# Second-choice sends one group behind the first ones, and blocks closed without GpSimd's DRAIN, in a two-FFN mixture-of-experts layer on one core

## The chip, the cores and the metric

The program runs on one core of one Trainium2 chip. The time is the device time of one execution in microseconds (us); of several executions the median counts. Lower is better.

## The reference

The input is x, 8 x 1024 tokens of 128 features. Three residual steps follow one another, and the first and the last are the same FFN with the same weights:

```python
x = x + 0.5 * ffn(layernorm(x))
x = x + attn(layernorm(x))
x = x + 0.5 * ffn(layernorm(x))

def ffn(x):                                   # x: 8192 x 128, 16 experts, top 2
    scores = softmax(x @ gate_w + gate_b)
    top_vals, top_idx = top_k(scores, 2)
    cw = (one_hot(top_idx, 16) * top_vals[..., None]).sum(axis=1)
    a = silu(x @ w1[e] + b1[e]) * (x @ w3[e] + b3[e])         # 176 wide, for each e
    y = einsum('teh,ehd,te->td', a, w2, cw) + cw @ b2
    z = silu(x @ sw1 + sb1) * (x @ sw3 + sb3) @ sw2 + sb2     # shared expert, 352 wide
    return y + z
```

The attention is linear: q and k go through elu + 1, kv = sum over the tokens of k v for each of 16 heads of 8, out = q kv, and a projection.

## The kernel before, in words

The 8192 tokens are 64 tiles of 128 tokens, in 8 groups of 8 tiles. They stay in SBUF (`xa`) from beginning to end. The program has six stages, each in a `phase`: front 0, experts 0, attention, front 1, experts 1, combine. Each stage is one `nc.Block()`, in which every engine has its own instruction stream and waits on semaphores by hand. At the end of a block all engines meet. Then `phase` clears the stage's semaphores (L71, `clear_and_free_semaphores`, done by GpSimd) and all engines meet again (L72, `all_engine_barrier`).

**front** (twice, n = 0 and 1) normalizes the tokens, computes the gate, finds both experts of each token, computes the shared expert on TensorE, and sends each token's row of 130 floats (128 features, a destination and a weight) to the table `xs` in HBM, once for the first choice and once for the second. There a region belongs to each expert. A send is one indirect DMA of 128 rows, issued by GpSimd (POOL) at L316; a group of one choice is eight of them. Both fronts issue 128. Both choices are sent from the same rows of SBUF, `xrow`: the first choice goes with destination `dest0` and weight 0.5/sum, and only when all eight first sends of the group have landed may VectorE (DVE) overwrite these two columns. That is `rewrite(g)` (L444 to L452): a wait on `sent0`, two small instructions (L449, L451), and the semaphore `rewrote`.

DVE, ScalarE, TensorE and POOL run on in steps s = -1 to 9. In step s they do the gate of group s and the shared expert of group s - 1, which is cut in six parts m. DVE's step (L526 to L563) reads, in this order: `shifts(s+1)` (L374, needs GpSimd's `scales`), `largest(s)`, `indices(s)`, three of six `gates` with `outs` between them, `hot(s)` (L409), `moments(s+2)`, `gates`, `sums(s)`, `variances(s+2)` (L369 is its last), `gates`, `outs`, `places(s)`, whose last instruction writes the slots of the group (L442), `gates`, `low` twice (L457), and as its last `rewrite(s-2)`.

GpSimd's stream in a front (L326 to L341): three `scales` (L323, one power of -1/2 of the variances of a group; it waits for `variances`), and then for each g the first sends of group g (wait on the slots of g), `scales(g+3)`, and the second sends of group g - 2 (wait on `rewrote`). Only after all sends have landed does it come to the end of the block. SyncE (SP) loads weights in front 0, and at the end copies 16 padding tiles in `xs` (L269).

**experts** takes 144 tiles of 128 rows in pairs: SP loads them (L860), TensorE transposes and multiplies, and GpSimd scatters each result tile to `ys` with one indirect DMA (L873). **attention** and **combine** read `ys` with DMAs of SP (L1060, L1265).

A block begins at L204 (front), L846 (experts), L1056 (attention) and L1259 (combine): what the program issues at the block's end carries these line numbers in the profile.

Of the kernel before, what the change touches and what calls it, by code (L numbers as in the profile page):

```python
# [32 lines left out]
GROUPS = 8  # L33
# [107 lines left out]
def front(nc, k, sb, ps, n, xa, xs, w=None):  # L141

    with phase(nc) as sem, ExitStack() as ctx:
# [57 lines left out]

            return slice(g * GT, (g + 1) * GT)

        with nc.Block() as block:  # L204
            @block.sync
            def _(sp):
                if n == 0:
# [64 lines left out]
            @block.gpsimd  # L272
            def _(pool):
                if n == 0:
                    pool.memset(k.ident[:], 0.0)
                    pool.memset(k.tri[:], 1.0)
                    pool.memset(k.blockdiag[:], 1.0)
                    pool.memset(k.onesb[:], 1.0)
                    pool.memset(k.nhalf[:], -0.5)
                    pool.memset(k.ones_e[:], 1.0).then_inc(tail, 1)  # L280
                    pool.wait_ge(tail, 1)
                    pool.affine_select(out=k.ident[:], in_=k.ident[:], compare_op=ALU.not_equal,
                                       fill=1.0, base=0, pattern=[[-1, P]], channel_multiplier=1
                                       ).then_inc(consts, 1)
                    pool.affine_select(out=k.tri[:], in_=k.tri[:], compare_op=ALU.is_ge, fill=0.0,
                                       base=-1, pattern=[[1, P]], channel_multiplier=-1)
                    heads = k.blockdiag[:].rearrange("p (a c) -> p a c", c=HEAD_DIM)
                    pool.affine_select(out=heads, in_=heads, compare_op=ALU.is_ge, fill=0.0,
                                       base=0, pattern=[[-HEAD_DIM, D // HEAD_DIM], [0, HEAD_DIM]],
                                       channel_multiplier=1).then_inc(consts, 1)  # L290
                    pool.wait_ge(consts, 2)
                    pool.affine_select(out=heads, in_=heads, compare_op=ALU.is_ge, fill=0.0,
                                       base=HEAD_DIM - 1,
                                       pattern=[[HEAD_DIM, D // HEAD_DIM], [0, HEAD_DIM]],
                                       channel_multiplier=-1)
                    pool.iota(k.iota_e[:], pattern=[[1, E]], base=0, channel_multiplier=0,
                              allow_small_or_imprecise_dtypes=True)
                    pool.iota(k.iota_j[:], pattern=[[P, 2]], base=0, channel_multiplier=1,
                              allow_small_or_imprecise_dtypes=True)
                    pool.iota(k.region[:], pattern=[[REGION, E]], base=0, channel_multiplier=0,  # L300
                              allow_small_or_imprecise_dtypes=True).then_inc(consts, 1)
                    pool.memset(k.zero[:], 0.0)
                    pool.memset(k.pad_tail[:], 0.0).then_inc(consts, 1)
                    pool.wait_ge(consts, 4)
                    pool.iota(k.pad_tail[:, :, 0:1].bitcast(I32).rearrange("p j a -> p (j a)"),
                              pattern=[[P, PADS]], base=TOKENS * K_TOP, channel_multiplier=1
                              ).then_inc(tail, 1)
                pattern = [[2 * GT * P, GROUPS], [2, GT]]
                pool.iota(dest0, pattern=pattern, base=0, channel_multiplier=2 * GT)
                pool.iota(dest1[:].rearrange("p (b i) -> p b i", i=GT), pattern=pattern, base=1,  # L310
                          channel_multiplier=2 * GT).then_inc(dests, 1)
                pool.wait_ge(dests, 1)

                def send(g, q, done):
                    for i in range(g * GT, (g + 1) * GT):
                        pool.indirect_dma_start(  # L316
                            xs, bass.IndirectOffsetOnAxis(slot[:, q, i:i + 1], 0), xrow[:, i, :],
                            None).then_inc(done, 16)

                def scales(g):  # L320
                    pool.wait_ge(var, g + 1)
                    wait(pool, xhr, 2 * (g - 2))
                    pool.tensor_tensor(rs[g % 3][:], ve[g % 2][:], k.nhalf[:], ALU.pow  # L323
                                       ).then_inc(rstd, 1)

                for g in range(3):  # L326
                    scales(g)
                for g in range(GROUPS + 2):
                    if g < GROUPS:
                        pool.wait_ge(slots, g + 1)  # L330
                        pool.wait_ge(weighted, g + 1)
                        pool.wait_ge(xhr, 2 * g + 2)
                        pool.sem_inc(passed, 1)
                        send(g, 0, sent0[g % 3])
                    if g + 3 < GROUPS:
                        scales(g + 3)
                    if g >= 2:
                        pool.wait_ge(rewrote, g - 1)
                        pool.sem_inc(passed, 1)
                        send(g - 2, 1, sent1)  # L340
                pool.wait_ge(sent1, 16 * TILES)  # L341

            @block.vector
            def _(dve):
# [181 lines left out]
                def step(s):  # L526
                    m, new, gating = 6 * (s - 1), s + 2 < GROUPS, 0 <= s < GROUPS
                    if 0 <= s < GROUPS - 1:
                        shifts(s + 1)
                    if gating:  # L530
                        largest(s)
                        indices(s)
                    gates(m)
                    if s == GROUPS:
                        tables()
                    gates(m + 1)
                    outs(2 * (s - 1) - 1)
                    if s == GROUPS:
                        tables_out()
                    gates(m + 2)  # L540
                    if gating:
                        hot(s)
                    if new:
                        moments(s + 2)
                    gates(m + 3)
                    if gating:
                        sums(s)
                    if new:
                        variances(s + 2)
                    gates(m + 4)  # L550
                    outs(2 * (s - 1))
                    if gating:
                        places(s)
                    gates(m + 5)
                    if gating:
                        if n == 0:
                            weight_low(2 * s)
                        low(2 * s)
                        low(2 * s + 1)
                        if n == 0:  # L560
                            weight_low(2 * s + 1)
                    if s >= 2:
                        rewrite(s - 2)  # L563

                if n == 0:
                    for r in range(4):
# [27 lines left out]
                for s in range(1, GROUPS + 2):  # L594
                    step(s)
# [215 lines left out]
def experts(nc, k, sb, ps, n, xs, ys):  # L811

    with phase(nc) as sem, ExitStack() as ctx:
# [28 lines left out]
            for j in range(TAIL, last):  # L843
                step(j, j)

        with nc.Block() as block:  # L846
            @block.sync
            def _(sp):
                def load(first, free):
# [160 lines left out]
def attention(nc, k, sb, ps, xa, ys):  # L1010
# [3 lines left out]
    with phase(nc) as sem, ExitStack() as ctx:  # L1014
# [19 lines left out]
        s = {m: sem(f"t_{m}") for m in names}  # L1034
# [18 lines left out]
        v_of = p_kv[:].rearrange("p a (t n) -> p (a t) n", n=2 * D)[:, :, D:2 * D]  # L1053
        q_of = p_q[:].rearrange("p a n -> p (a n)")

        with nc.Block() as block:  # L1056
            @block.sync
            def _(sp):
                def load(g, gv):
# [193 lines left out]
def combine(nc, sb, rs, ys, out):  # L1253

    with phase(nc) as sem, ExitStack() as ctx:
        yt = [sb(f"c_yt{r}", [P, GT, 2 * D], ctx=ctx) for r in range(4)]
        in_ready = [sem(f"c_in{r}") for r in range(GROUPS)]
        half, ysum, stored = sem("c_half"), sem("c_ysum"), sem("c_stored")
        with nc.Block() as block:  # L1259
            @block.sync  # L1260
            def _(sp):
                for g in range(GROUPS):
                    if g >= 4:
                        sp.wait_ge(ysum, g - 3)
                    sp.dma_start(yt[g % 4][:], ys[:, g]).then_inc(in_ready[g], 16)  # L1265
                sp.wait_ge(stored, 16 * GROUPS)

            @block.vector
            def _(dve):
                for g in range(GROUPS):  # L1270
                    dve.wait_ge(in_ready[g], 16)
                    dve.tensor_tensor(rs[:, g * GT:(g + 1) * GT], rs[:, g * GT:(g + 1) * GT], yt[g % 4][:, :, 0:D], ALU.add  # L1272
                                      ).then_inc(half, 1)
                    dve.wait_ge(half, g + 1)
                    dve.tensor_tensor(rs[:, g * GT:(g + 1) * GT], rs[:, g * GT:(g + 1) * GT], yt[g % 4][:, :, D:2 * D], ALU.add  # L1275
                                      ).then_inc(ysum, 1)

            @block.scalar
            def _(act):
                for g in range(GROUPS):  # L1280
                    act.wait_ge(ysum, g + 1)
                    act.dma_start(out[:, g], rs[:, g * GT:(g + 1) * GT]).then_inc(stored, 16)
# [26 lines left out]
```

## Time and profile before

| | us |
|---|---|
| median of 3 runs | 1052.64 |
| lowest, highest | 1049.37, 1054.99 |
| profiled execution, its own time | 1053.46 |
| its span, first to last instruction | 1051.7 |
| TensorE busy | 803.1 (76% of the span) |
| GpSimd busy | 590.6 (56%) |
| VectorE busy | 588.3 (56%) |
| ScalarE busy | 468.7 (45%) |

In the profile, times are from the start of the span. A line of a timeline gives the start and the duration in us, the engine, the line of the kernel, the operation and the tiles, and in brackets the idle time of the engine before it with what ended it ("issue" stands for idle time for which the profile shows no releaser).
### The profile page before, as it was taken

The numbers are of one execution on the slowest core, as the hardware profiler recorded it, in microseconds if no ns is written. First come the engines' busy times: TensorE is split into PE (matmuls) and PEld (weight loads), VectorE is DVE, ScalarE is ACT, GpSimd is POOL, SyncE is SP. The second block draws the span as 40 slices with busy tenths as digits, with TensorE's granted clock in tenths as the row PEclk, the third lists the DMA queues.
The fourth block names the chain that finished last, engine by engine and source line by source line (L and its number), as shares of the span: only waits on it lengthen the run. The fifth ranks groups of instructions, "written<-read, shape, count | busy, mean of one in ns | idle before, by whom it ended". The sixth has DMA issues, their size and how long they took to land. (4 is left out here: it accounts for less than half of the span.)

```text
span 1051.7 us, 20394 instructions
## 1 busy us (share of the span) xinstructions
PE 803.1 (76%) x5408; PEld 718.9 (68%) x5409; DVE 588.3 (56%) x1989; ACT 468.7 (45%) x926; POOL 590.6 (56%) x600
## 2 busy tenths in 40 slices
PE   2899999607999999328989489999810999999910
PEld 2677787507999999326777468877710999999910
DVE  6577766404555555256885477776600555555526
ACT  3466564104555555134664256575200555555500
POOL 2446777753777777532220146677774477776730
PEclk9999999858999999757999679998965999999965
DMA  9812221312333333232200001111231333333339
GB/s 276 118 38 60 66 63 51 95 43 77 101 103 101 103 104 96 68 133 81 80 0 1 0 22 34 40 49 49 61 88 39 89 101 101 103 101 103 94 132 374
DMA packets 82819, 90.42 MB, mean 86 GB/s; under 512 B 20414, under 2 KB 69451, under 8 KB 80715
## 3 DMA queue, kind: packets, MB, share of 16 engines
q1 hardware_dynamic: 63052, 45.42, 16.9%
q0 software_dynamic: 17408, 35.95, 10.2%
q10 hardware_dynamic: 2304, 8.39, 2.0%
q8 instruction: 26, 0.43, 0.2%
q14 instruction: 29, 0.24, 0.1%
HBM read 47.46 MB, written 44.37 MB: 87 GB/s over the span
## 5 line engine op out<-in xcount | busy, mean ns | idle before, releaser
L873 POOL DMA_INDIRECT ys<-e_y,e_x x288 | 275.8, 958 | 139.8 <-issue 87.8
L316 POOL DMA_INDIRECT xs<-f_xrow,f_slot x256 | 252.8, 987 | 87.6 <-issue 75.3
L992 PE MATMUL e_py<-w,e_at 97*128 (+1 forms) x1152 | 152.2, 274 | 0.0
L992 PEld LDWEIGHTS e_py<-w,e_at 97*128 97x128 f32 (+1 forms) x1152 | 139.9, 191 | 0.2 <-issue 0.2
L917 ACT ACTIVATE e_xth<-e_px 128x256 fp32r<-128x256 f32 x144 | 55.2, 384 | 171.4 <-PE e_px L956 171.4
L897 DVE TENSOR_TENSOR e_a<-e_pu,e_sil 128x352 f32<-128x352 f32 x144 | 75.5, 525 | 96.9 <-ACT e_sil L923 91.6
L956 PE MATMUL e_px<-ident,e_x 128*128 128x128 f32 x288 | 57.7, 282 | 90.7 <-DMA e_x<-xs 86.4
L904 DVE TENSOR_SCALAR e_y<-e_py,e_x 128x128 f32<-128x128 f32 x288 | 87.8, 346 | 58.0 <-PE e_py L992 57.9
L756 PEld LDWEIGHTS f_pz<-sw,f_gated 128*128 128x128 f32 (+1 forms) x768 | 102.6, 195 | 9.3
L649 ACT ACTIVATE f_sil<-f_phg,sb 128x512 f32<-128x512 f32 (+1 forms) x96 | 64.7, 685 | 97.9 <-PE f_phg L742 97.6
L468 DVE SCALAR_TENSOR_TENSOR f_gated<-f_phg,sb,f_sil 128x512 f32<-128x512 f32 (+1 forms) x96 | 71.7, 747 | 63.8 <-ACT f_sil L649 54.4
L923 ACT ACTIVATE e_sil<-e_pu 128x352 f32<-128x352 f32 x144 | 66.7, 463 | 89.9 <-PE e_pu L969 89.9
L967 PE MATMUL e_pu<-w13h,e_xth 128*128 x288 | 106.7, 370 | 0.0
L756 PE MATMUL f_pz<-sw,f_gated 128*128 128x128 f32 (+1 forms) x768 | 102.7, 278 | 0.0
L956 PEld LDWEIGHTS e_px<-ident,e_x 128*128 128x128 f32 x288 | 36.0, 145 | 94.9 <-DMA e_x<-xs 89.7
L742 PE MATMUL f_phg<-f_xth,sw13h 128*128 128x512 f32 (+1 forms) x192 | 89.7, 467 | 10.3 <-ACT f_sil L649 9.1
L969 PE MATMUL e_pu<-w13h,e_xtl 128*128 x288 | 93.7, 325 | 0.0
L968 PE MATMUL e_pu<-w13l,e_xth 128*128 x288 | 93.6, 325 | 0.0
L929 ACT ACTIVATE e_at<-e_pa 96x512 f32<-96x512 f32 x144 | 85.5, 594 | 1.6 <-PE e_pa L979 1.6
L979 PE MATMUL e_pa<-ident,e_a 128*96 128x128 f32 x576 | 86.2, 272 | 0.0
L742 PE MATMUL f_phg<-f_xtl,sw13h 128*128 128x512 f32 (+1 forms) x192 | 79.3, 413 | 0.0
L742 PE MATMUL f_phg<-f_xth,sw13l 128*128 128x512 f32 (+1 forms) x192 | 78.8, 410 | 0.0
(160 smaller groups left out, 1431.7 us busy)
## 6 DMA issues: line engine op xcount, KB each, us to landing
e_x<-xs SPq DMA_DIRECT2D x288, 65.0 KB
t_yt<-ys SPq DMA_DIRECT2D x8, 1024.0 KB, 4.9
c_yt<-ys SPq DMA_DIRECT2D x8, 1024.0 KB, 10.4
ys<-e_y,e_x POOLq DMA_INDIRECT x288
xa<-in_attn_x ACTq DMA_DIRECT2D x8, 512.0 KB, 10.3
xs<-f_xrow,f_slot POOLq DMA_INDIRECT x256, 2.4
out<-xa ACTq DMA_DIRECT2D x8, 512.0 KB
f_raw<-in_ffn_w SPq DMA_DIRECT2D x32, 88.0 KB
```

Source lines behind the costliest of these rows:

```text
L316: pool.indirect_dma_start(xs, bass.IndirectOffsetOnAxis(slot[:, q, i:i + 1], 0), xrow[:, i, :], None).then_inc(done, 16)
L742: last = pe.matmul(p_hg[(2 * m + g) % 3][0:wd], w_[:, cols], x_[c % 3][:], start=q == 0, stop=q == 2)
L756: last = pe.matmul(p_z[c % 2][:, tok], gated[c % 2][0:wd, f, tok], k.sw2[0:wd, f], start=f == 0 and q == 0, stop=f == 2, skip_group_check= ...
L873: pool.indirect_dma_start(ys, bass.IndirectOffsetOnAxis(xin[r][:, t, D:D + 1].bitcast(I32), 0), y[r][:, t, :], None).then_inc(sent[r], 16)
L904: last = dve.tensor_scalar(y[s][:, t], p_y[j % 2][:, t * D:(t + 1) * D], xin[s][:, t, D + 1:D + 2], None, ALU.mult)
L929: act.activation(at[r][0:A0], p_a[0:A0], ACT.Copy).then_inc(turned, 1)
L956: last = pe.transpose(p_x[:, t * P:(t + 1) * P], xin[s][:, t, 0:D], k.ident[:])
L967: pe.matmul(o, xth[r][:, tok], k.w13h[:, cols], start=True, stop=False)
L968: pe.matmul(o, xth[r][:, tok], k.w13l[:, cols], start=False, stop=False)
L969: last = pe.matmul(o, xtl[r][:, tok], k.w13h[:, cols], start=False, stop=True)
L979: last = pe.transpose(p_a[0:A0, q * P:(q + 1) * P], a[r][:, t, o:o + A0], k.ident[:])
L992: last = pe.matmul(p_y[r][:, t * D:(t + 1) * D], at[r][0:rows_, q], w2, start=c == 0, stop=c == 1, skip_group_check=True)
```

## The change

In GpSimd's stream the second sends of group g - 1, in place of g - 2, follow the first sends of group g. The loop is one turn shorter. In DVE's step `rewrite(s-2)` stands ahead of `hot(s)` and no longer at the end. All four `nc.Block()` get `no_gpsimd_drain=True`: at the block's end GpSimd issues no DRAIN, and the engines meet by semaphores alone. `phase`, with its clearing of semaphores and the barrier behind it, is as before.

```diff
-        with nc.Block() as block:
+        with nc.Block(no_gpsimd_drain=True) as block:
...
                 for g in range(3):
                     scales(g)
-                for g in range(GROUPS + 2):
+                for g in range(GROUPS + 1):
                     if g < GROUPS:
                         pool.wait_ge(slots, g + 1)
                         pool.wait_ge(weighted, g + 1)
...
                         send(g, 0, sent0[g % 3])
                     if g + 3 < GROUPS:
                         scales(g + 3)
-                    if g >= 2:
-                        pool.wait_ge(rewrote, g - 1)
+                    if g >= 1:
+                        pool.wait_ge(rewrote, g)
                         pool.sem_inc(passed, 1)
-                        send(g - 2, 1, sent1)
+                        send(g - 1, 1, sent1)
                 pool.wait_ge(sent1, 16 * TILES)
...
                     gates(m + 2)
+                    if s >= 2:
+                        rewrite(s - 2)
                     if gating:
                         hot(s)
...
                         low(2 * s + 1)
                         if n == 0:
                             weight_low(2 * s + 1)
-                    if s >= 2:
-                        rewrite(s - 2)
```

The first line of the diff stands for the blocks of front, experts, attention and combine.

## Rows read from the trace of the kernel before

**Rows 1.** Busy time by stretch: the ends of both fronts, and the start of experts 0.
```profile
core 0: us, PE busy (x) PEld busy (x) DVE busy (x) ACT busy (x) POOL busy (x), PEclk, DMA share, GB/s
205.40:230.50 25.10, 0.00 (x0) 0.00 (x0) 0.00 (x0) 0.00 (x0) 19.16 (x20) 0.56 0.21 66
230.50:251.60 21.10, 9.15 (x56) 8.59 (x57) 5.09 (x12) 4.67 (x11) 0.00 (x1) 0.64 0.22 55
...
774.40:803.30 28.90, 0.00 (x0) 0.00 (x0) 0.14 (x2) 0.00 (x0) 22.04 (x23) 0.50 0.16 53
```

**Rows 2.** The page's costliest groups of instructions: GpSimd's scatter of both stages.
```profile
L873 POOL DMA_INDIRECT ys<-e_y,e_x x288 | 275.8, 958 | 139.8 <-issue 87.8
L316 POOL DMA_INDIRECT xs<-f_xrow,f_slot x256 | 252.8, 987 | 87.6 <-issue 75.3
```

**Rows 3.** Timeline of POOL in front 0, around its last idle times, and its last send.
```profile
65.81 0.95 POOL L316 DMA_INDIRECT xs<-f_xrow,f_slot  x1 [0.30 <-issue]
72.10 1.67 POOL L323 TENSOR_TENSOR f_rs<-f_ve,nhalf 128x8 f32<-128x8 f32 x1 [5.33 <-DVE f_ve L369]
77.10 1.30 POOL L316 DMA_INDIRECT xs<-f_xrow,f_slot  x1 [3.33 <-DVE f_slot L442]
...
86.65 0.96 POOL L316 DMA_INDIRECT xs<-f_xrow,f_slot  x1 [0.30 <-issue]
92.97 1.67 POOL L323 TENSOR_TENSOR f_rs<-f_ve,nhalf 128x8 f32<-128x8 f32 x1 [5.36 <-DVE f_ve L369]
94.83 1.03 POOL L316 DMA_INDIRECT xs<-f_xrow,f_slot  x1 [0.20 <-issue]
...
229.50 0.96 POOL L316 DMA_INDIRECT xs<-f_xrow,f_slot  x1 [0.30 <-issue]
```

**Rows 4.** Timeline of POOL in front 1, the same places, and its last `scales`.
```profile
645.61 1.67 POOL L323 TENSOR_TENSOR f_rs<-f_ve,nhalf 128x8 f32<-128x8 f32 x1 [4.61 <-DVE f_ve L369]
649.44 1.34 POOL L316 DMA_INDIRECT xs<-f_xrow,f_slot  x1 [2.15 <-DVE f_slot L442]
...
658.99 0.95 POOL L316 DMA_INDIRECT xs<-f_xrow,f_slot  x1 [0.30 <-issue]
664.93 1.67 POOL L323 TENSOR_TENSOR f_rs<-f_ve,nhalf 128x8 f32<-128x8 f32 x1 [4.99 <-DVE f_ve L369]
...
709.99 1.67 POOL L323 TENSOR_TENSOR f_rs<-f_ve,nhalf 128x8 f32<-128x8 f32 x1
...
802.28 0.96 POOL L316 DMA_INDIRECT xs<-f_xrow,f_slot  x1 [0.31 <-issue]
```

**Rows 5.** Timeline of DVE: `hot` of step 2, and late places in front 1.
```profile
67.87 0.48 DVE L409 TENSOR_TENSOR f_onehot<-iota_e,f_idx 128x128 bf16<-128x128 f32 x2
...
711.69 0.17 DVE L374 SCALAR_TENSOR_TENSOR f_nm<-f_mv,f_rs 128x8 f32<-128x8 f32 x1 [2.39 <-POOL f_rs L323]
...
739.03 0.48 DVE L409 TENSOR_TENSOR f_onehot<-iota_e,f_idx 128x128 bf16<-128x128 f32 x2
...
774.28 0.17 DVE L449 SCALAR_TENSOR_TENSOR f_xrow<-f_rec,f_wtop 128x8 f32<-128x8 f32 x1 [7.04 <-DMA xs<-f_xrow,f_slot]
```

**Rows 6.** GpSimd's DRAINs by line: duration ns min/median/max, first and last start us.
```profile
L204 POOLq DRAIN  x2: 4642/4684/4727, 232.0 to 805.1; - x2
...
L846 POOLq DRAIN  x2: 3647/3651/3655, 439.3 to 1013.0; - x2
...
L1056 POOLq DRAIN  x1: 1627/1627/1627, 550.6 to 550.6; - x1
...
L71 POOLq DRAIN  x6: 77/105/169, 236.8 to 1051.2; - x6
```

**Rows 7.** Timeline of POOL: its last compute instruction in attention.
```profile
550.46 1.65 POOL L1081 TENSOR_TENSOR t_rs<-t_ve,nhalf 128x8 f32<-128x8 f32 x1 [9.58 <-DVE t_ve L1132]
```

**Rows 8.** All sends of both fronts: duration ns min/median/max, and issue to landing.
```profile
L316 POOL DMA_INDIRECT xs<-f_xrow,f_slot x256: 954/958/1642, 30.1 to 802.3; - x128
...
DMA to landing us min/median/max: 2.3/2.4/7.4
```

More of the change, by code:

```diff
@@ L844, in steps @@
                 step(j, j)
-        with nc.Block() as block:
+        with nc.Block(no_gpsimd_drain=True) as block:
             @block.sync
@@ L1054, in attention @@
         q_of = p_q[:].rearrange("p a n -> p (a n)")
-        with nc.Block() as block:
+        with nc.Block(no_gpsimd_drain=True) as block:
             @block.sync
@@ L1258, in combine @@
         half, ysum, stored = sem("c_half"), sem("c_ysum"), sem("c_stored")
-        with nc.Block() as block:
+        with nc.Block(no_gpsimd_drain=True) as block:
             @block.sync
```

## The prediction

> **What bounds the kernel now.** TensorE is busy for most of the span, but the share is an average over stages, so I went first to the ends of the stages. The table by stretch shows the end of front 0 with POOL alone at work: from 205.4 to 230.5 us no other compute engine has an instruction, and POOL has 20. In front 1 the same holds from 774.4 to 803.3 us, but for two tiny DVE instructions [rows 1]. What stops the next stage is thus a queue of sends on GpSimd. The page's groups give their price: 256 sends at L316 of 987 ns on the mean, each behind 0.30 us of issue [rows 2], so a send takes 1.26 us and a group of eight about 10.15 us.
>
> GpSimd's timeline then tells whether that queue was ever idle when it could have worked. In front 0 POOL is without a gap from 94.83 us, where the first second-choice send starts, to its last send, which ends at 229.50 + 0.96 = 230.46 us [rows 3]. Thirteen groups of sends and two `scales` of 1.87 us fit there: 13 x 10.15 + 3.7 = 135.7 us, and 230.46 - 94.64 = 135.8 us. In front 1 the last send ends at 803.24 us [rows 4]. So each front ends when POOL's total work ends. A microsecond of POOL idleness removed ahead of the queue is a microsecond off the stage. The experts' stages are POOL's too (144 scatters of 0.958 + 0.30 us each [rows 2]), and the change leaves them alone.
>
> **The change part by part.**
>
> *Second sends one group earlier.* No send is added or removed; the order changes. I replay POOL's stream with the old durations.
>
> Front 0: after the first sends of group 1 (last one ends at 66.76) POOL waits for DVE's variances until 72.10 and does `scales(4)`, to 73.77 [rows 3]. The second sends come behind `scales` in the new order as well, so these 5.33 us stay. Next it waited 3.33 us for the slots of group 2. The new order has the second sends of group 0 here. They need `rewrite(0)`, which now stands ahead of `hot` in DVE's step 2, and that `hot` ran at 67.87 [rows 5]: ready. They start after the usual 0.20 us, fill the gap and push the first sends of group 2 to about 84.1 us. These end at 94.3, by when the variances that POOL awaited until 92.97 us are long there; the wait of 5.36 us is gone too. From there on everything is queued, as before. Gain: 3.33 - 0.20 + 5.36 = 8.5 us; the last send ends at 222.0.
>
> Front 1: the same two gaps are 649.44 - 647.28 = 2.16 us and 664.93 - 659.94 = 4.99 us [rows 4]. Gain: 2.16 - 0.20 + 4.99 = 7.0 us, to 796.3. Earlier gaps in both fronts stay, since there is nothing that may be sent. Sum for the order: **15.4 us**, paid in full, because the tail that it shortens has nothing else in it. DVE's last work needs the landed first sends of group 7: 774.28 in front 1 before, behind a wait of 7.04 us [rows 5]. It gets some 3 us later (below), still 19 us ahead of the end.
>
> *What the move makes late.* One more group of second sends (10.15 us) now stands ahead of `scales(5)` to `scales(7)`, against 8.5 or 7.0 us won: they come 1.6 us later in front 0 and 3.2 us in front 1. `scales(7)` of front 1 was already what DVE waited for, 2.39 us [rows 5]; it will wait about 3 us more, and ScalarE and TensorE behind it. Cost nothing: DVE was done with all but the last `rewrite` before 767.3 us (774.28 less the 7.04 us of waiting), and 770 is still far from 796. If that cover went, the price would be those 3 us.
>
> *`rewrite` earlier in DVE's step.* The two instructions of 0.17 us change place; on DVE they cost nothing new. The wait on `sent0` moves ahead of `hot`, three `gates` and `places`, so a late first send would now hold up TensorE's feed and the slots. In front 1, step 7, `hot` stood at 739.03 [rows 5], about 742 with the delay above. By my replay, `scales(7)` ends at 714.9, then come the second sends of group 3 and the first ones of group 5, to 735.2, landed by 736.7 (2.4 us from an issue to its landing [rows 8]). The margin is 5 us, and in front 0 more. Nothing.
>
> *No DRAIN at a block's end.* The removed DRAINs of GpSimd took 4.64 and 4.73 us behind the fronts and 3.65 us behind each experts' stage [rows 6], with all engines waiting: 16.7 us in all. In attention the 1.63 us lay beside TensorE, so it is worth nothing. But `phase` clears semaphores with another GpSimd DRAIN at L71, which the change keeps and which all engines wait for at L72. Today it takes 0.08 to 0.17 us [rows 6], because the one before it did the waiting. What does a DRAIN wait for? In attention it started at 550.6 and lasted 1.63 us, to 552.2; POOL's last instruction ran 550.46 to 552.11 [rows 7]. It waits until the engine has finished. Behind the sends something of 3.6 to 4.7 us is unfinished that the trace doesn't name, and the DRAIN of L71 will find it unfinished as well. Bounds: 0 us gained if all of it moves, 16.7 if none does. I take the lower one, as the attention row is the nearest that tells what a DRAIN does, plus what of L71's own DRAIN and of the meeting overlaps, 0.1 to 0.3 us at four ends: **0.6 us**.
>
> The Trainium skill (Perfetto Trace Analysis, "Sequencer-only Instruction (DRAIN, etc)") draws DRAIN as an instruction of the sequencer alone, whose profiled time is execution; by that the removed time would be saved and the sum would gain 16.7 us there. The row of attention speaks against it.
>
> Sum: 15.4 + 0.6 = 16.0 us. The profiled execution took 1053.46 (span 1051.7), which gives 1037.4; it stood 0.8 above the median of the runs, so the median comes to **1036.6 us**. About 0.5% (5.3 us) is what a measurement of this kernel can tell from no change.
>
> **The rivals.**
>
> *A, the DRAIN's time is really gone.* The wait belongs to the block's DRAIN, or passes before L71 asks. For it: two different times, 4.7 and 3.65, each repeated within 0.1 us, look like fixed routines rather than a leftover. Against it: the DRAIN of attention, and that of L71 has nothing to hide behind. Time: 1036.6 + 0.6 - 16.7 = 1020.5 us. Chance 0.14.
>
> *B, sends get slower beside DVE.* The gain is 12 sends that no longer run in the quiet tail but in time shared with DVE. Over both fronts the mean is 987 against a median of 958 ns, and the longest took 1642 [rows 2, 8]; in the quiet tail they take 0.96. If each of the 12 took the longest time, 12 x 0.68 = 8.2 us would be given back: 1044.8 us. Against it, most sends beside DVE already take 0.96. Chance 0.09.
>
> [...]
>
> *C, slower: the wait on landed sends closes a loop.* DVE stops at `rewrite(g)` in step g + 2 until the first sends of g have landed; behind it stand `hot` and the slots of g + 2, for which POOL then waits. From `hot` to the next send it was 77.10 - 67.87 = 9.2 us [rows 3, 5]; with 1.4 us of landing POOL would sit idle 10.6 us for each of groups 3 to 7, in both fronts: 106 - 16 us, or about 1143. It decides only if POOL has less than 10.6 us of other work between the first sends of g and those of g + 2. It has three groups of sends and two `scales`, 34 us. Chance 0.03.
>
> *D, the tail doesn't shrink,* since another end (SP's padding copies, or the landing) holds the block. Every other engine is silent there, so 0.02, about 1052.
>
> **How the numbers follow.** The forecast has 0.72. Its own range is 1031 to 1042: 1.5 us for the replay, 1.2 for the DRAINs' overlap, and the spread of the runs, which was 3 us to either side. To hold 8 in 10 the range takes in B, up to 1046, and goes to 1029 for a DRAIN that is partly gone; A, C and D stay outside. Faster by over 0.5% (below 1047.4) are the forecast, A and B: 0.95. Within 0.5% is D: 0.02. Slower is C: 0.03.
>
> **What the profile after would show.** POOL in front 0: a send in place of the gap at 73.8 us, no gap from then on, the last send near 222 us; in front 1 near 796. The quiet stretch behind DVE's last instruction falls by as much. `scales(7)` of front 1 ends near 715, and DVE's wait for it at L374 is longer than 2.4 us. No POOL DRAIN at L204 and L846, but those of L71 with 3.6 to 4.7 us behind fronts and experts. Wrong would be: short DRAINs at L71 (A), sends whose mean is well above 987 ns (B), or gaps of POOL ahead of a send released by L442 late in a front (C).

## The result, and the profile after

| | median us | lowest, highest | runs |
|---|---|---|---|
| before | 1053.82 | 1049.37, 1055.17 | 4 |
| changed | 1019.34 | 1018.50, 1020.17 | 4 |

The ratio is 0.968, with a 95% interval from 0.965 to 0.971: 34 us faster. The forecast was 1036.6 with a range from 1029 to 1046, so the result lies outside the range, on the fast side. It lies 1.2 us from rival A (1020.5), which had a chance of 0.14; how much of that nearness is luck is said with the table below. The profiled execution took 1019.16 us, its span is 1017.4 us.

The sends come first. GpSimd's timeline in front 0, at the places of [rows 3]:

```profile
70.01 1.67 POOL L323 TENSOR_TENSOR f_rs<-f_ve,nhalf 128x8 f32<-128x8 f32 x1 [5.51 <-DVE f_ve L369]
71.87 1.03 POOL L316 DMA_INDIRECT xs<-f_xrow,f_slot  x1 [0.20 <-issue]
...
91.90 1.67 POOL L323 TENSOR_TENSOR f_rs<-f_ve,nhalf 128x8 f32<-128x8 f32 x1
93.77 1.03 POOL L316 DMA_INDIRECT xs<-f_xrow,f_slot  x1 [0.19 <-issue]
...
218.45 0.95 POOL L316 DMA_INDIRECT xs<-f_xrow,f_slot  x1 [0.30 <-issue]
```

Behind `scales(4)` a send starts after 0.20 us where there were 3.33 us of waiting, and ahead of `scales(5)` (91.90) there is no bracket at all: the 5.36 us are gone. The 5.5 us ahead of `scales(4)` have stayed, as replayed. The last send ends at 219.4 us, 11.1 earlier. Of these 2.3 us aren't the change's: already the fourth `scales` stands at 49.09 us here and at 51.35 in the profile of before, while the first weights load. In the other runs below it stands between 48.0 and 50.5, in the old order (49.41 without the DRAIN) as in the new one (49.30 with it), so this is spread of single executions.

The same places in front 1, as in [rows 4]:

```profile
624.99 1.67 POOL L323 TENSOR_TENSOR f_rs<-f_ve,nhalf 128x8 f32<-128x8 f32 x1 [5.14 <-DVE f_ve L369]
626.86 1.19 POOL L316 DMA_INDIRECT xs<-f_xrow,f_slot  x1 [0.20 <-issue]
...
648.05 1.76 POOL L323 TENSOR_TENSOR f_rs<-f_ve,nhalf 128x8 f32<-128x8 f32 x1
...
693.32 1.67 POOL L323 TENSOR_TENSOR f_rs<-f_ve,nhalf 128x8 f32<-128x8 f32 x1
...
775.57 0.96 POOL L316 DMA_INDIRECT xs<-f_xrow,f_slot  x1 [0.30 <-issue]
```

The price of a send is unchanged, as the page's groups show beside [rows 2]: still 987 ns on the mean in the fronts.

```profile
L873 POOL DMA_INDIRECT ys<-e_y,e_x x288 | 275.8, 958 | 130.9 <-issue 88.9
L316 POOL DMA_INDIRECT xs<-f_xrow,f_slot x256 | 252.8, 987 | 82.5 <-issue 75.4
```

The ends of the fronts, by stretch, beside [rows 1]. The stretch of front 0 still holds DVE's last four instructions, which end at 203.2 us, so its quiet part is 16.2 us, where there were 25.1. In front 1 it is 18.5, where there were 28.9; about 5 us of this difference are the earlier end, and 5 are DVE's last `rewrite`, which comes that much later in the stage (the prediction had 3).

```profile
201.80:219.40 17.60, 0.00 (x0) 0.00 (x0) 1.33 (x4) 0.00 (x0) 13.38 (x14) 0.63 0.28 80
758.00:776.50 18.50, 0.00 (x0) 0.00 (x0) 0.00 (x0) 0.00 (x0) 14.23 (x15) 0.50 0.16 54
```

Then the DRAINs. Those of GpSimd at L204 and L846 [rows 6] are no longer there, and this is what stands at L71 and L72 now (duration ns min/median/max, first and last start us):

```profile
L71 POOLq DRAIN  x6: 72/100/170, 221.2 to 1016.9; - x6
...
L72 POOLq DRAIN  x6: 40/45/51, 221.9 to 1017.2; - x6
```

The wait that I expected to reappear at L71 is not there. The whole difference of both profiled executions, by stage, from the starts and ends of the lines that bound them:

| stretch | before | after | won |
|---|---|---|---|
| front 0, to the end of its last send | 230.46 | 219.40 | 11.1 |
| from there to the experts' first instruction (L884) | 7.48 | 2.91 | 4.6 |
| experts 0, to the end of the last scatter | 199.87 | 199.71 | 0.2 |
| from there to the first load of attention (L1060) | 6.01 | 2.33 | 3.7 |
| attention | 145.68 | 143.53 | 2.2 |
| front 1, from L309 to the end of its last send | 213.74 | 208.65 | 5.1 |
| to L884 | 7.86 | 2.99 | 4.9 |
| experts 1 | 200.39 | 201.10 | -0.7 |
| to combine's first load (L1265) | 6.01 | 2.34 | 3.7 |
| combine | 34.2 | 34.4 | -0.2 |

The four gaps between stages give 16.9 us, which is the length of the removed DRAINs, 16.7. The fronts give 16.2, of which 2.3 are the early loads. So 13.9 us are left for the order of the sends, where the replay said 15.4. Rival A came so near in part by luck: its sum had neither the 2.3 us of early loads nor the 2.2 of attention, and they are set off in part by the 1.5 us that the order gave less and by the 0.7 of experts 1.

### The profile page after: what moved, and what is told of

Same layout as the page of the kernel before. It is cut to its first block and busy times, and to the rows that moved or that the text cites. A ratio compares the mean times of both kernels' runs of the same rounds, so it can differ in the third digit from the quotient of the medians.

```text
span 1017.4 us, 20412 instructions
## 1 busy us (share of the span) xinstructions
PE 800.3 (79%) x5408; PEld 717.5 (71%) x5409; DVE 588.2 (58%) x1989; ACT 468.7 (46%) x926; POOL 590.6 (58%) x600
```

## The experiments

There were three theories of what the removed DRAIN had done. *Leftover*: GpSimd still has work of its own behind its last send, which passes with time, and a DRAIN only waits for it. *Routine*: a plain DRAIN itself works something off for the sends issued since the last one, whenever it is called. *Fixed price*: a plain DRAIN costs the same each time. The first two runs split the change.

**Order alone.** The changed kernel with `nc.Block()` in place of `nc.Block(no_gpsimd_drain=True)` four times.

> The changed kernel with plain blocks again, so that GpSimd's DRAIN stands at each block's end as before; the order of the sends is the new one. Both theories on the DRAIN expect the same here: the order alone gives 15.4 us by the replay, about 16 as the profile of the changed kernel reads, so 1037 to 1039 beside 1053 for the kernel before. The POOL DRAINs at L204 and L846 are back at 4.7 and 3.65 us. A gain of clearly less than 13 us would say that the order and the DRAIN share a part.

1036.46 us against 1051.68 for the kernel before: ratio 0.9855 with a 95% interval from 0.9828 to 0.9882, 15.2 us (12 to 18). Its DRAINs and last send of front 1:

```profile
L204 POOLq DRAIN  x2: 3993/4036/4078, 221.3 to 787.7; - x2
...
L846 POOLq DRAIN  x2: 3652/3654/3655, 428.8 to 995.9; - x2
```

```profile
784.96 0.95 POOL L316 DMA_INDIRECT xs<-f_xrow,f_slot  x1 [0.30 <-issue]
```

Front 1 starts here at 579.09 (L309), so it takes 206.8 us to the end of this send, exactly the replay's number (796.3 - 589.5). The DRAIN behind the fronts came back, but at 4.0 us and not at the 4.7 that I had expected: the new order shortens it too. Over two fronts this is 1.3 of the 15.2 us.

**No DRAIN alone.** The kernel before with the four blocks closed without it.

```diff
-        with nc.Block() as block:
+        with nc.Block(no_gpsimd_drain=True) as block:
```

> The kernel before with the four blocks closed without GpSimd's DRAIN, and the old order. If the removed 16.7 us are gone and nothing takes their place (the changed kernel's DRAINs at L71 are 0.1 us), the time is 1053 - 17 = 1036. If the place of the sends matters for it, the sum of both single gains is off the 34 us of the whole change by more than 3 us.

1036.43 us against 1051.68: ratio 0.9844 [0.9822, 0.9867], 15.3 us (14 to 19). So each half gains by itself, and neither needs the other. Together they make 15.2 + 15.3 = 30.5 us, where the whole change gave 34.5 us, and 32.5 when it was measured again (below). The first is over the 3 us that I had set as the mark for a dependence. But each of these gains is uncertain by about 3 us, so the runs neither show a dependence nor rule one out; the shorter DRAINs of the new order would make the sum of the halves the larger one, by 1.3 us.

**The DRAIN later, and twice.**

```diff
                 pool.wait_ge(sent1, 16 * TILES)
+                for r in range(5):
+                    pool.tensor_tensor(rs[0][:], ve[0][:], k.nhalf[:], ALU.pow
+                                       ).then_inc(late, 1)
+                    pool.wait_ge(late, r + 1)
...
                 for r in range(RING):
                     pool.wait_ge(sent[r], 32 * (PAIRS // RING))
+                pool.drain()
```

> The kernel before (plain blocks). In both fronts GpSimd does five powers of 1.67 us between the landing of all sends and the block's DRAIN; in both experts' stages it issues one DRAIN more ahead of the block's own. Theory 'leftover': GpSimd has work of its own behind its last send, which passes with time; then the DRAIN at L204 is under 0.3 us after 8 us of other work. Theory 'routine': a plain DRAIN itself works off something for each send issued since the last one, when it is called; then it stays at 4.6 to 4.7 us. Of the two DRAINs behind the experts, 'leftover' and 'routine' expect the first near 3.65 and the second under 0.2 us; a third theory, that a plain DRAIN always costs this much in a program with sends, expects 3.65 for both.

The line numbers have moved: L205 is the block of the fronts, L884 the additional DRAIN of the experts, L851 that of their block.

```profile
L205 POOLq DRAIN  x2: 4627/4634/4642, 238.1 to 817.6; - x2
L851 POOLq DRAIN  x2: 40/40/40, 449.7 to 1030.1; - x2
L884 POOLq DRAIN  x2: 3652/3654/3655, 446.1 to 1026.4; - x2
```

```profile
229.37 8.52 POOL L344 TENSOR_TENSOR f_rs<-f_ve,nhalf 128x8 f32<-128x8 f32 x5 [1.43 <-DMA xs<-f_xrow,f_slot]
```

8.5 us of other work, after all sends have landed, take nothing off the DRAIN: 4.63 us. *Leftover* fails here, at least where GpSimd is busy with something else. Of two in a row the second takes 0.04 us, so *fixed price* fails too. (The one execution took 1066.92 us, 15 more than before; the 2 x 8.5 us of powers account for it.)

**The number of sends.** A wait for what has been sent and a DRAIN, at more places of the kernel before:

```diff
                         pool.wait_ge(rewrote, g - 1)
                         pool.sem_inc(passed, 1)
+                        if g == GROUPS + 1:
+                            pool.wait_ge(sent1, 16 * (TILES - GT))
+                            pool.drain()
...
                                 y[r][:, t, :], None).then_inc(sent[r], 16)
+                    for r in range(RING):
+                        pool.wait_ge(sent[r], 32 * i + 32)
+                    pool.sem_inc(passed, 1)
+                    pool.drain()
```

> The kernel before (plain blocks), with more DRAINs of GpSimd: in the fronts one ahead of the last group of sends, when the other 120 have landed, and in the experts' stages one at the end of each of nine turns, when the 16 sends of that turn have landed. 'Routine' expects durations that go with the number of sends since the last DRAIN: in the fronts about 4.4 us for 120 and 0.3 us for the 8 that are left to the block's, in the experts' stages about 0.4 us in each turn (3.65 / 9), and next to nothing for the block's own. 'Leftover' expects the same length, 3.6 to 4.7 us, wherever a DRAIN comes right behind sends, however few they are.

L342 is the new one in the fronts and L883 that of the experts' turns:

```profile
L204 POOLq DRAIN  x2: 701/701/701, 235.2 to 831.9; - x2
L342 POOLq DRAIN  x2: 3979/3986/3993, 219.1 to 815.8; - x2
L849 POOLq DRAIN  x2: 46/46/46, 468.1 to 1066.5; - x2
L883 POOLq DRAIN  x18: 1352/1352/1362, 273.4 to 1064.5; - x18
```

0.70 us for 8 sends and 1.35 for 16, eighteen times the same: the length goes with the number, and in the experts' stages the block's own DRAIN has nothing left. Idle time takes nothing off it either: in the first turn the last scatter ends at 271.8 us and the DRAIN starts at 273.4, so GpSimd had 1.6 us of waiting, and the DRAIN still took 1.35. But the shares that I had expected, in proportion to the whole, are wrong: 16 sends cost 1.35 and not 0.4 us, and nine such DRAINs cost 12.2 us where one behind all 144 costs 3.65. (The one execution took 1103.28 us.) So a second run took more sizes.

```diff
                         send(g - 2, 1, sent1)
+                    if g in ((3, 7), (2, 8))[n]:
+                        for r in range(3):
+                            pool.wait_ge(sent0[r], 16 * GT * ((min(g, 7) - r) // 3 + 1))
+                        pool.wait_ge(sent1, 16 * GT * (g - 1))
+                        pool.drain()
```

> The kernel before (plain blocks) with DRAINs of GpSimd inside the fronts, each behind a wait for all sends so far: in front 0 after 48 sends, then after 64 more, and the block's own after the last 16; in front 1 after 32, then 88, then 8. Measured so far: 0.70 us for 8, 1.35 for 16, 3.99 for 120, 4.68 for 128 and 3.65 for 144 in the experts' stages. If the routine goes through the sends one by one but only a limited number is ever left for it, 16 cost 1.35, 32 some 2.7, and 48, 64 and 88 all near 4 us. If it grows evenly with the number, 32, 48, 64 and 88 lie on a line between 1.35 and 3.99, at 1.9, 2.4, 2.8 and 3.3.

Its DRAINs inside the fronts, L345, after 48, 64, 32 and 88 sends, one row for each stretch of time (the one execution took 1072.41 us):

```profile
L345 POOLq DRAIN  x1: 3988/3988/3988, 127.5 to 127.5; - x1
...
L345 POOLq DRAIN  x1: 5269/5269/5269, 217.4 to 217.4; - x1
...
L345 POOLq DRAIN  x1: 2672/2672/2672, 685.5 to 685.5; - x1
...
L345 POOLq DRAIN  x1: 7234/7234/7234, 806.6 to 806.6; - x1
```

The lengths of all these runs and of the kernel before, by the number of sends (or scatters) that GpSimd issued since its last plain DRAIN:

| sends | 8 | 16 | 32 | 48 | 64 | 88 | 120 | 128 | 144 |
|---|---|---|---|---|---|---|---|---|---|
| us | 0.70 | 1.35 | 2.67 | 3.99 | 5.27 | 7.23 | 3.99 | 4.68 | 3.65 |

The 120 are those ahead of L342, the 128 and 144 those of whole stages in the old order. Up to 88 it is close to a straight line: 6.53 us for the 80 sends between 8 and 88, or 0.082 us for a send. That is neither of the two forms that I had written down: there is no flattening below 88, and then the time falls. By 120 sends part of what a DRAIN would have to work off is gone without one. What takes it off, and why 128 sends in the new order leave 4.0 us and not 4.7, is open.

**The remaining gaps.** The profile of the changed kernel still shows GpSimd idle ahead of `scales(3)` and `scales(4)`. This version sends the second choices of group 0 one turn earlier, and from group 2 on puts `scales` behind them.

```diff
-                    if g + 3 < GROUPS:
+                    if g < 2:
                         scales(g + 3)
-                    if g >= 1:
-                        pool.wait_ge(rewrote, g)
+                    if g != 1:
+                        pool.wait_ge(rewrote, max(g, 1))
                         pool.sem_inc(passed, 1)
-                        send(g - 1, 1, sent1)
+                        send(max(g - 1, 0), 1, sent1)
+                    if 2 <= g < GROUPS - 3:
+                        scales(g + 3)
...
-                    if s >= 2:
+                    if s >= 4:
                         rewrite(s - 2)
...
                         variances(s + 2)
+                    if s == 1:
+                        rewrite(0)
...
                             weight_low(2 * s + 1)
+                    if s == 2:
+                        rewrite(1)
```

> The changed kernel with GpSimd's remaining idle times in the fronts filled: rewrite(0) moves to step 1 (behind variances), rewrite(1) to the end of step 2, the second sends of group 0 go out right behind the first ones and scales(3), those of group 1 behind the first sends of group 2, and from group 2 on the second sends stand ahead of scales. If a front ends when GpSimd's total work ends, it ends 16 x 10.15 + 5 x 1.87 = 171.8 us after its first send: 202 in front 0 (where the other engines last until about 205, so 14 us are won there, and not more) and 762 in front 1, which wins 14 us: together 1019 - 28 = 991 us. The rival: now that scales come 10 us later, DVE waits for them and the slots of the next group come too late, GpSimd's gaps come back, and the gain is under 10 us (over 1009).

The changed kernel was run once more beside it.

> The changed kernel once more, on the chip of the run without gaps: 1019 us, as measured, to compare with it.

| beside the same runs of before (1052.02) | median us | ratio |
|---|---|---|
| changed kernel | 1019.57 | 0.9687 [0.9654, 0.9719] |
| without the gaps | 1011.58 | 0.9613 [0.9581, 0.9646] |

8 us better than the changed kernel, where I had expected 28. GpSimd's timeline in front 0:

```profile
47.96 1.67 POOL L323 TENSOR_TENSOR f_rs<-f_ve,nhalf 128x8 f32<-128x8 f32 x1 [7.79 <-DVE f_ve L371]
...
73.73 1.29 POOL L316 DMA_INDIRECT xs<-f_xrow,f_slot  x1 [2.19 <-DVE f_slot L444]
...
107.36 0.96 POOL L316 DMA_INDIRECT xs<-f_xrow,f_slot  x1 [0.79 <-DVE f_xrow L453]
```

```profile
682.58 0.96 POOL L316 DMA_INDIRECT xs<-f_xrow,f_slot  x1 [1.76 <-DVE f_xrow L453]
...
706.33 0.96 POOL L316 DMA_INDIRECT xs<-f_xrow,f_slot  x1 [1.77 <-DVE f_xrow L453]
```

GpSimd is still idle for 14.7 us between the first and the last send of front 0 and for 8.8 us in front 1, where the profile of the changed kernel has 18 and 12 (counting waits above 0.4 us). The expected sum counted no idle time at all, but the 7.79 us ahead of `scales(3)` can't be filled in this order: the second sends of group 0 stand behind it, and `rewrite(0)` comes after the same `variances`. In addition the second sends, now early, wait for `rewrite` themselves, 0.8 us here and 1.8 in front 1. That is the new wait in place of the old one. The rival of the expectation, a gain under 10 us, had the right number, but late slots, its mechanism, are the smaller part: 4.6 us of GpSimd's waits in both fronts, against 7.4 for `rewrite` and 12.5 ahead of `scales(3)`. This version is the fastest of this study.

## Why the prediction was wrong

*What bounds the kernel*, and *second sends one group earlier*: right in mechanism, and in size within the spread of the runs. The replay said 15.4 us; the order alone gave 15.2 with 1.3 of it from shorter DRAINs, which the prediction didn't have, so 13.9 for the sends. Front 0 was to end at 222.0, less the 2.3 us of early loads 219.7, and ended at 219.4; front 1 was to take 206.8 us and took 206.8 with the DRAINs and 208.7 in the changed kernel, where GpSimd's idle times are 0.8 us longer and its sends 1.2 us longer in sum.

*What the move makes late*: `scales(7)` of front 1 ends 127.1 us after the start of the stage, where the replay said 125.4. DVE's waits for `scales` rose from 3.0 to 7.0 us over the program, the longest from 2.4 to 3.8. They cost nothing, since GpSimd's queue ends later anyway.

*`rewrite` earlier in DVE's step*: in the changed kernel DVE waits for landed sends once, 7.0 us, as before: the harmless last one. (With the DRAINs, and in the second profile of the changed kernel, there is one more wait, of 0.6 and 0.3 us.) Rival C's loop never closed. Rival B fell with the unchanged 987 ns, rival D with the shorter quiet ends.

*No DRAIN at a block's end*: this is the step that failed. "It waits until the engine has finished" was read off the DRAIN of attention, which had one power in front of it and no send. From this I went on to "the DRAIN of L71 will find it unfinished as well" and took the lower bound, 0.6 us, of a term that could be 16.7. The runs show in its place a time of the plain DRAIN itself: up to 88 sends it is 0.08 us for each send since the last plain DRAIN, and 3.65 to 4.7 us behind 120 to 144, and neither the landing of the sends nor 8.5 us of other work takes it away. I call that work of its own; what it consists of is not shown. The DRAIN of L71 came behind 128 or 144 sends without a plain one and took 0.10 to 0.17 us, and the plain one at L72 behind it took 0.04 to 0.05. So what comes with the clearing of the semaphores costs no such time and leaves nothing to the next DRAIN. Whether the DRAIN of L71 or the clearing behind it does that was not separated. Nothing was lost with the removed DRAIN, because each block waits for all its sends by semaphores.

I had a sign of it in the rows: both lengths, 4.7 and 3.65 us, repeated within 0.1 us [rows 6]. Rival A had named it and got 0.14; the nearest row was the same instruction in another situation. The section of the Trainium skill that the prediction names ("Sequencer-only Instruction (DRAIN, etc)" in Perfetto Trace Analysis) draws the profiled time of a DRAIN as its execution. That agrees with the DRAINs behind sends, whose 16.7 us went with them; it does not tell of the wait in the 1.63 us of attention's, which ended with the power.

## What to carry to other kernels

A DRAIN of GpSimd behind many indirect DMAs is not free, even if all have landed: here it took 3.65 to 4.7 us at each of four ends. Where every DMA is waited for by a semaphore and a clearing of semaphores follows, as here, try to close the stage without it. If one queue runs without a gap to the end of its stage, its early idle times are the whole gain that an order can bring; here a replay of the queue, row by row, came within 2 us of the measured gain. And if a term has bounds of 0.6 and 16.7 us, a row of the same instruction in another situation doesn't choose between them.

## What I had not expected

Attention became 1.3 to 2.2 us shorter, though nothing in it was touched. TensorE's granted clock by stretches of 20 us, the second and third from attention's first load on. In the kernel before:

```profile
463.82:483.82 20.00, 13.17 (x43) 10.11 (x42) 9.52 (x28) 8.74 (x15) 6.33 (x4) 0.59 0.24 88
483.82:503.82 20.00, 19.47 (x106) 15.72 (x105) 16.18 (x31) 12.06 (x26) 5.57 (x3) 0.89 0.19 60
```

In the changed kernel:

```profile
444.35:464.35 20.00, 13.17 (x46) 10.32 (x44) 10.21 (x28) 8.74 (x15) 7.01 (x4) 0.67 0.23 88
464.35:484.35 20.00, 18.75 (x110) 15.17 (x110) 16.76 (x36) 13.93 (x28) 4.88 (x3) 0.97 0.28 97
```

In the first 20 us of the stage the clock is at 0.50 (1.2 GHz) in both kernels. It rises from there towards 1.00 (2.4 GHz) earlier in the changed one. With the order alone it is 0.59 and 0.89 as before, and attention takes 145.8 us; with only the DRAINs removed it is 0.67 and 0.94, and 144.4 us. In front 1 it goes the other way: the second stretch of 20 us has 0.79 with DRAINs and 0.73 without, and the stage is 1.8 us longer with the same order. I take the difference for the moment at which the clock steps up. In attention the shorter pause ahead of the stage may have shifted it, but ahead of front 1 TensorE's pause is the same, 8.7 us before and 8.8 after, so there this explanation doesn't hold. The cause is open; it was not tried by itself.
